# Tensor product stage of a four-layer graph network: the index load issued by ScalarE, the hidden weight rows loaded by two DMAs with a repeated source

## What is computed

```python
r = edge_vec / norm(edge_vec);  sh1 = SQRT3 * r
xs, xd = x[edge_src], x[edge_dst]                 # 32 features each, 8 scalars and 8 vectors
s1 = concat(xs[:, :8], xd[:, :8]);  v1 = concat of the 8 x 3 vector parts
w  = relu(emb @ fc1_w1 / ...) @ fc1_w2 / ...      # 512 weights per edge, from 16 hidden values
s_t, v_t = products of s1, v1, sh1 with w         # first product, weights from 16 hidden values
w2 = relu(emb @ fc2_w1 / ...) @ fc2_w2 / ...      # 384 weights per edge, from 16 other hidden values
scal, gates, vecs = products of s_t, v_t, sh1 with w2
edge_out = concat(tanh(scal), vecs * tanh(gates)) * edge_weight
x = layer_norm(x + segment_sum(edge_out, edge_dst))
```

## Time and profile before

| | us |
|---|---|
| median of three runs (lowest, highest) | 32074.3 (32060.67, 32092.36) |
| the profiled execution's own time | 31756.59 |
| its span | 31754.5 |
| PE busy over the span | 16766.2 (53%) |
| DVE busy | 16097.6 (51%) |
| POOL busy | 13376.2 (42%) |
| ACT busy | 4841.3 (15%) |

### The profile page before, as it was taken

The page is one execution under the profiler, slowest core; times in us unless marked ns, Lnnn a source line. Parts: engine busy times, 40 slices in busy tenths (PEclk is TensorE's granted clock), DMA queues, the critical chain, the costliest instruction groups (busy, mean ns, idle before and its releaser), DMA issues. The chain is left out here.

```text
span 31754.5 us, 470714 instructions
## 1 busy us (share of the span) xinstructions
PE 16766.2 (53%) x108690; PEld 10500.2 (33%) x108691; DVE 16097.6 (51%) x32216; ACT 4841.3 (15%) x11885; POOL 13376.2 (42%) x13048
## 2 busy tenths in 40 slices
PE   7344444445555549996100000005777777777777
PEld 5233333323333339994000000004333333333333
DVE  9444444455555544443111112995666666666666
ACT  4111111111111112221000000000222222222222
POOL 0355555556666650000566666650333333333332
PEclk9555555555555555555555555555777777777777
DMA  2444444432222232110322232221333344333333
GB/s 65 102 122 120 119 121 122 121 80 59 59 59 58 58 97 97 38 38 14 73 80 81 80 80 78 70 57 53 94 93 94 92 95 95 94 94 93 94 93 88
DMA packets 2914657, 2637.09 MB, mean 83 GB/s; under 512 B 1449983, under 2 KB 2276029, under 8 KB 2911618
## 3 DMA queue, kind: packets, MB, share of 16 engines
q1 hardware_dynamic: 2297198, 2104.11, 25.1%
q0 software_dynamic: 412544, 241.53, 5.3%
q10 hardware_dynamic: 203668, 275.37, 3.2%
HBM read 2070.87 MB, written 537.90 MB: 82 GB/s over the span
## 5 line engine op out<-in xcount | busy, mean ns | idle before, releaser
L2507 POOL DMA_INDIRECT rows_x<-x_table,index x3125 | 2952.3, 945 | 7322.8 <-DMA index<-in_src 6560.3
L1559 POOL DMA_INDIRECT rows_dram<-rows,place_now x3125 | 2991.4, 957 | 4900.0 <-DVE rows L1487 3887.4
L758 POOL DMA_INDIRECT rows<-split_table,index x3125 | 2986.9, 956 | 3632.0 <-DMA index<-in_src 2677.0
L874 POOL DMA_INDIRECT rows<-x_table,index x3125 | 3297.0, 1055 | 1718.5 <-issue 914.3
L2214 DVE TENSOR_TENSOR first<-banks,h 128x768 f32<-128x768 f32 x2500 | 1945.5, 819 | 2338.8 <-remote 1622.1
L1499 PE MATMUL banks<-row_pieces,hot_turned 128*128 x3125 | 390.2, 289 | 4173.0 <-issue 2661.1
L1487 DVE TENSOR_REDUCE rows<-banks 128x108 f32<-128x324 f32 x1250 | 490.6, 434 | 4022.3 <-issue 2712.7
L2222 DVE TENSOR_TENSOR second<-banks,h 128x768 f32<-128x768 f32 x2500 | 1959.7, 820 | 1028.9 <-DMA rows_dram<-rows,place_now 463.7
L192 PE MATMUL banks<-rows,onehot 128*128 128x65 f32 (+1 forms) x9375 | 1845.8, 372 | 417.2 <-issue 244.3
L567 PE MATMUL banks<-counts,low_turned 128*128 128x98 f32 x6250 | 1803.9, 436 | 413.3 <-ACT counts L555 289.4
L192 PEld LDWEIGHTS banks<-rows,onehot 128*128 128x128 f32 (+1 forms) x9375 | 1679.7, 268 | 508.6 <-issue 272.0
(11 more groups left out here) (469 smaller groups left out, 32948.6 us busy)
## 6 DMA issues: line engine op xcount, KB each, us to landing
key_row<-dst_rows SPq DMA_DIRECT2D x1250, 320.0 KB
h<-hidden_dram SPq DMA_DIRECT2D x10000, 40.0 KB
acc_moved<-dst_rows SPq DMA_DIRECT2D x625, 320.0 KB
src_row<-in_src_rows SPq DMA_DIRECT2D x625, 320.0 KB
hot_turned<-turned_dram SPq DMA_DIRECT2D x1250, 160.0 KB
hot_dram<-onehot SPq DMA_DIRECT2D x625, 160.0 KB
turned_dram<-hot_turned SPq DMA_DIRECT2D x625, 160.0 KB
a_dram<-a ACTq DMA_DIRECT2D x625, 160.0 KB
```

The lines of the kernel that those rows point to most:

```text
L758: nc.gpsimd.indirect_dma_start(out=m["rows"][j][:, t * SPLIT:(t + 1) * SPLIT], out_offset=None, in_=m["split_table"], in_offset=bass.Indir ...
L874: nc.gpsimd.indirect_dma_start(out=m["rows"][j][:, t * C2:t * C2 + F], out_offset=None, in_=m["x_table"], in_offset=bass.IndirectOffsetOnA ...
L1559: nc.gpsimd.indirect_dma_start(out=m["rows_dram"], out_offset=bass.IndirectOffsetOnAxis(ap=m["place_now"][j][:, t:t + 1], axis=0), in_=m[" ...
L2507: nc.gpsimd.indirect_dma_start(out=m["rows_x"][j][:, t * F:(t + 1) * F], out_offset=None, in_=m["x_table"], in_offset=bass.IndirectOffsetO ...
```

## The change

SyncE no longer loads the index tile, except for the first five groups. ScalarE issues it at the end of each of its turns, for the group five ahead, after a wait for `copied` of the turn's own group. And each of h1 and h2 is loaded by one DMA of 128 rows, whose source is the 16 DRAM rows with a leading dimension of 8 that repeats them; VectorE's wait counts 32 for a group, no longer 256.

```diff
--- before.py
+++ after.py
@@ -2113,9 +2113,8 @@
 
     def sp_group(sp, i, j, again):
         g = SLOTS * i + j
-        if again:
-            sp.wait_ge(s["copied"][j], ONE + i)
-        sp.dma_start(m["index"][j][:, :], m["src"][:, bass.ds(g * T, T)]).then_inc(s["indexed"][j], 16)
+        if not again:
+            sp.dma_start(m["index"][j][:, :], m["src"][:, bass.ds(g * T, T)]).then_inc(s["indexed"][j], 16)
         if again or j >= 3:
             sp.wait_ge(s["owned"], ONE + g - 1)
         sp.dma_start(m["hot_turned"][j % 3][:, :], m["turned_dram"][bass.ds(g, 1)].rearrange("g p e -> (g p) e")).then_inc(s["turned_in"][j], 16)
@@ -2128,10 +2127,8 @@
         if again:
             sp.wait_ge(s["doubled"], ONE + CHUNKS * (g - SLOTS + 1))
         for k, name in enumerate(("h1", "h2")):
-            for u in range(U8):
-                sp.dma_start(m[name][j][K16 * u:K16 * (u + 1), :],
-                             m["hidden_dram"][bass.ds(g, 1), K16 * k:K16 * (k + 1), :].rearrange("g h e -> (g h) e")
-                             ).then_inc(s["hidden_in"][j], 16)
+            sp.dma_start(m[name][j][:, :], m["hidden_dram"][bass.ds(g, 1), K16 * k:K16 * (k + 1), :].broadcast_to([U8, K16, T * P])
+                         ).then_inc(s["hidden_in"][j], 16)
         if again:
             sp.wait_ge(s["hot_whole"], ONE + g - SLOTS + 1)
             sp.sem_inc(s["going_sp"], 1)
@@ -2142,6 +2139,11 @@
         act.wait_ge(s["turned"], ONE + 2 * (SLOTS * i + j))
         rows = m["rows_x"][j][:, :].rearrange("p (t b w) -> p t b w", t=T, b=4)
         nc.scalar.copy(blocks()[:, :, :, K16:K16 + U8], rows).then_inc(s["copied"][j], 1)
+
+    def act_index(act, i, j):
+
+        act.wait_ge(s["copied"][j], ONE + i)
+        act.dma_start(m["index"][j][:, :], m["src"][:, bass.ds((SLOTS * i + j) * T, T)]).then_inc(s["indexed"][j], 16)
 
     def act_hot(act, i, j):
 
@@ -2187,6 +2189,8 @@
             act_hot(act, *at(i, j, -1))
         if there(i, j, 2):
             act_inputs(act, *at(i, j, 2))
+        if there(i, j, 0) and there(i, j, SLOTS):
+            act_index(act, i + 1, j)
 
     def dve_front(dve, i, j):
 
@@ -2208,7 +2212,7 @@
 
         width = HALVES[half][1]
         if half == 0:
-            dve.wait_ge(s["hidden_in"][j], 32 * U8 * (i + 1))
+            dve.wait_ge(s["hidden_in"][j], 32 * (i + 1))
         for pair in range(2):
             dve.wait_ge(s["brackets"], ONE + CHUNKS * (SLOTS * i + j) + 2 * half + pair + 1)
             nc.vector.tensor_tensor(m["first"][2 * half + pair][:, :].rearrange("p (k e) -> p k e", k=2), bank_pair(4 + 2 * pair, width),
```

## The result

| | before | changed |
|---|---|---|
| median us (lowest, highest; runs side by side) | 32083.33 (32060.67, 32100.51; 4) | 32441.47 (32378.0, 32490.84; 4) |
| ratio, 95% interval | | 1.0111 (1.0092 to 1.013) |
| the profiled execution | 31756.59 | 32490.84 |

The change costs 358 us, 1.1%. The forecast was 31886; the time lies inside the range and beside the rival called "slower" (32455).

A forecast was written before the change was run, and what follows sets the result against it. Bound: engines stopped during POOL's five gathers, 3.91 us a turn. Quietness (up to -0.52 us), partly taken back by the place, taken as -0.3 x 625 = -188: 32074.3 - 188 = 31886 us; range about 31400 to 32550.

The forecast's parts named there:

- slower: Rival, last stage: gather fixed where the three engines depend on each other most; +381 us, 32455 us; chance 0.27.
- What bounds the kernel: Last stage: engines see each other's results late during POOL's five gathers; this is TensorE's 3.91 us idle a turn.
- SyncE is not the bound: Last stage: SyncE issues 22 DMAs a turn but waits 1.9 us a turn for `gated`, so it keeps up.
- SyncE's h loads at 0 us: SyncE's turn: 16 issues become 2, saving 7.8 us a turn, but SyncE only waits longer: 0 us.
- the slack of 28 us: Last stage: h issued by 27015.4 is first multiplied two turns later, at 27043.79.
- the rule of the eight engines: Merged h loads: a leading repeat of 8 keeps a DMA on at most 8 engines; 8.0 of 15.29 us, fits.
- My rival of the missed aim: Rival: h loads on few DMA engines reach into the gather, so it is not quiet; +1.41 us a turn, 32955; chance 0.07.
- ScalarE's issue at 0 us: Index load behind ScalarE's copy L2144: covered by 3.38 us, cost 0; without cover +300 us as upper end.
- The gather would start some 3 us behind L2144, once a turn, always there: POOL's gather after the change: starts some 3 us behind ScalarE's copy L2144, with SyncE silent for 2 us already.
- Nearer to the mild gather, since silence of SyncE is the one thing certain: Last stage's sum: -0.3 us a turn, -188 us, nearer the gather with 3.39 us TensorE idleness and SyncE silent at first.
- silence at -0.52 us a turn: Last stage: SyncE silent during every gather, TensorE idle 3.39 for 3.91 us a turn; -325 us.
- the place, priced at +0.61 us: Last stage: new gather position stops engines just before VectorE's product that TensorE needs; 4.52 for 3.91 us a turn, +381 us.

The follow-up runs named there:

- the first set: Runs trying the change's two parts apart: h loads merged alone, SyncE's index, ratio 1.0112 to the kernel before; with sixteen rows outermost 1.0055.
- the fourth: Set with lighter stops: kernel before 31760.61 us; changed kernel with index after first `units` 31619.67, with sixteen rows outermost as well 31551.2.
- the third: Set without stops: kernel before 26642.72 us; changed kernel with index after first `units` 26490.21, with sixteen rows outermost as well 26460.3.

## Why the prediction was wrong

**What bounds the kernel: right.** The stops behind the gathers were only concluded; now they are shown. One gather for five, or five split into two, two and one, shortens the turn by 3.3 to 3.5 us. That this was TensorE's 3.91 us of idleness was wrong: 1.2 us of it went, and 2.0 us came from its matmuls, which are faster when the stops are gone; the sum took their time as fixed. One reading was off as well: in the earlier trace rows ScalarE and VectorE are back 7.1 to 7.3 us behind the gather's start, TensorE only at 9.0. Not seen was the next bound close below: SyncE's list at 12 us, of which the change removes 7.8 us. "SyncE is not the bound" held only while the stops lasted.

**SyncE's h loads at 0 us: half right.** No engine's wait for h appears, the slack of 28 us held. But it was the wrong slack. I had the rule of the eight engines and asked of it only whether the traffic fits (8.0 of 15.29 us) and h comes in time. What it delayed was the small load behind it: index to gather 7.0 us for 2.7. The order with eight outermost has a part of the loss: 159 us in the first set with SyncE's index, 68 us in the fourth and 30 in the third with ScalarE's. My rival of the missed aim had them reach into the gather; they pushed the gather away instead.

**ScalarE's issue at 0 us: right.** The index alone by ScalarE at a better place is 199 us faster than the kernel before.

**"The gather would start some 3 us behind L2144, once a turn, always there": wrong as put.** With the index alone moved it is 2.2 us; in the changed kernel 6.5 us in the median and 2.7 to 7.6 in nine of ten, since the index load takes its time from the burst of h ahead of it.

**"Nearer to the mild gather, since silence of SyncE is the one thing certain": this is the step that failed.** SyncE is silent: of the sixteen issues of h 5.1 fell beside the average row of five gathers before, 0.2 of two do now. VectorE starts 11.2 operations in the nine us behind a gather, as forecast (some 10), for 6.0 before. But TensorE starts 45.5 matmuls, not over 50, for 48.7 before, and VectorE's second dip eats up what a shallower stop gives. Quietness was read off picked gathers that differed in their place as well, and nothing separated the two: with sixteen loads and SyncE busy all along, the index after `units` (0.9940) is faster than anything quiet at the turn's end (1.0023 to 1.0111). I priced silence at -0.52 us a turn, and no run shows a gain from it; the place, priced at +0.61 us (+381 us), came out at +358 us in the set of the result, +386 us with the index alone, and +73 us where the stops are lighter. So the rival "slower", to which I gave 0.27, had the mechanism: a gather fixed at a costly place, 2.4 us behind VectorE's `u` where it was 5.8. That its 381 us lie so close to 358 is luck in part: they are priced from one stop of a light set, and in the light set the same change costs 73 us. Its place was not exact either: the index alone has it (2.2 us behind the copy, 3 were forecast), the changed kernel not, and the stop hits the second product of the group in the timeline above, but in other turns other work.

**The scale.** I put the difference of 317.7 us between the profiled execution and the median down to nothing and shifted the sum by it. It was a sign that the stops vary from run to run, and that a term of 0.3 us a turn read from one execution is smaller than that.

**What stays open.** Why gathers in a row stop the engines' answers from about the third on, what makes the stops light, heavy or absent from one set to the next, and what share of the loss in the heavy sets belongs to the turns around the loop's branch: the changed kernel's first profile shows a surplus of 2.0 us there, less than the 2.8 of the kernel before in a lighter set.

## What to carry to other kernels

When all engines fall idle together at a fixed time behind a DMA-issuing engine's burst, first take the burst apart (leave part out, or split it with waits) before you move anything around it: here the split took the ratio from 0.9937 to 0.9264 (two sets), and the change at hand moved it to 1.0111. A load's new shape or queue is to be judged by the smallest, latest load that shares its DMA engines, not by its own consumer's slack. And where stops are periodic, moving an event changes what they hit: try the same line at two or three places of the turn, which took 31891, 32157 and 32429 us here (the last in another set). Measure the place by an engine's own step, not by one that the stop delays.

## What the runs showed of the hardware

- Five indirect gathers in a row, started 1.25 us apart, stop the three compute engines from about 3.5 to 7 us behind the first; two in a row with pauses of some 2 us don't, three do in part, four did each time. It is no fixed property: the same program ran in 26643 us in one set, without a stop, and the stages ahead, with gathers of their own, took 19053 us there for 22098 to 22267 in the windows shown of other sets.
- The issue order between queues gave no priority: an index load of 2.5 KB on ScalarE's queue took 7.0 us beside 655 KB of h on SyncE's, 2.75 us beside the same bytes in sixteen loads. These are times from issue to the gather's start.
- A stop is paid twice, once in idleness and once in slower matmuls behind it (1.66 us at 1.2 GHz for 0.93 us at 2.4 GHz), with the granted clock at 0.76 to 0.80 of full in the stage against 0.96 and 0.97 without stops.
